# An attention block and a quantised feed-forward network on one core: the opening of the kernel in another order, and four later places

## The chip, the core and the metric

The kernel runs on one core of one Trainium2 chip. A core has five engines that run side by side: PE (TensorE, matrix products), DVE (VectorE), ACT (ScalarE), POOL (GpSimd) and SP (SyncE, which here only issues DMA transfers). They meet through semaphores. Each engine works through its own list of instructions in order, so an instruction that waits holds up all that stand behind it. The metric is the device time of one execution in microseconds (us); lower is better.

## The reference

The input `x` is 16 batches of 100 tokens of 512 numbers; `ctx` is 16 batches of 361 rows of 256. All is float32.

```
x = x + attention(layernorm(x), ctx)
        q = xn @ Wq, k = ctx @ Wk, v = ctx @ Wv      16 heads of 128
        q, k = rmsnorm(q) * gq, rmsnorm(k) * gk
        softmax(q k^T / sqrt(128)) v, then @ Wo
x = x + ffn(layernorm(x))
        gate, up (4096 x 512), down (512 x 4096) as 4-bit codes with scales
        gelu(x @ gate^T) * (x @ up^T) @ down^T
```

## The kernel before, in words

Every float32 operand of a matrix product is split into a high and a low part (`..._hi`, `..._lo`), and each product is three passes: high by high, high by low, low by high (`matmul3`, line 399). The high part is a cast, mostly on ACT (`hi`, line 791); the low part is a subtraction on DVE (`lo`, line 1158) or POOL.

The attention part runs in 64 units. A unit is one batch with one quad of four heads. Four units with the same quad and four batches (`GB`) share their queries; `quad` counts these groups of four units from 0 to 15, `i` is the unit inside its group, and `v` the unit inside the 16 that belong to the same four batches. In a unit PE does, in this order: the scores of the unit, the keys of the next unit (`keys`), the transposes of the attention weights (`transpose_attn`, line 467), two products with the context rows (`attend`, lines 482 to 488), and the transposes of the next unit's keys (`transpose_keys`, line 459). Between these stand products that belong to the group: the queries of the next quad (`query`), the values and the outputs of the quad before (`value_of`, `output`). `attend` needs the transposed weights back from ACT (high part) and DVE (low part).

Before unit 0 there is an opening: four batches of `x` are loaded, normalised (`ln1_moments`, a reciprocal root by POOL in `ln_rstd`, `ln1_normalise`), transposed by PE (`norm_transposed`, line 498) and split (`norm_hi` on ACT, `ln1_lo` on DVE, semaphore `xl`). The key weights `wk` and the head weights `head_w` are split too (`head_hi` on ACT, `head_lo` on POOL, line 1809). The first query waits until all four batches are split.

The order on every engine is written out by hand, in one function per engine. In the unit loop the POOL splits the fresh head weights (`split_head`, lines 1697 and 1699) for products that PE takes soon after. The weights of the feed-forward network are decoded in steps that are put into the last attention units (`decode` on DVE, lines 1338 to 1349). SP issues the transfers in order too, with waits in between: a head weight is loaded into one of two buffers when the one in it has been split, and each split weight is stored to memory for later quads.

## Time and profile before

| | before |
|---|---|
| median of 3 runs | 2015.75 us (2015.48 to 2016.67) |
| the profiled execution, its own time | 2015.15 us |
| span of its instructions | 2013.4 us |
| PE busy | 1968.3 us, 98% of the span |
| DVE, ACT, POOL busy | 79%, 50%, 57% |
| mean granted clock of PE | 0.993 |

The profiled execution is 1.75 us longer than its span and 0.6 us under the median. PE stood still for about 45 us of the span. The rows below are from views that list instructions in order of time for one engine, with the idle time before each and what ended it, and from views that sum up a stretch.

### The profile page before, as it was taken

How to read it: one execution, taken by the hardware profiler on the slowest of the kernel's cores; microseconds unless marked ns; L12 is line 12 of the kernel's file. 1: busy time of each engine (PE TensorE's matmuls, PEld its weight loads, DVE VectorE, ACT ScalarE, POOL GpSimd, SP SyncE). 2: the span in 40 equal slices, each digit the busy share in tenths (PEclk: the TensorE clock that was granted, in tenths of full speed). 3: DMA queues.
4: the chain of work that ended last, by engine and by line, in shares of the span. 5: the costliest groups of instructions: out<-in, count | busy, mean ns of one | idle time of the engine just before them, and what ended most of it. 6: DMA issues, size and time to landing. Idle time of an engine off the chain costs nothing.

```text
span 2013.4 us, 34243 instructions
## 1 busy us (share of the span) xinstructions
PE 1968.3 (98%) x11504; PEld 1894.8 (94%) x11504; DVE 1596.6 (79%) x3034; ACT 1000.4 (50%) x2322; POOL 1152.1 (57%) x1305
## 2 busy tenths in 40 slices
PE   6999999999999999999999999989999999999998
PEld 5899899999999999999999999979999999999998
DVE  6777787778877778877788877888888888888875
ACT  4555455555555555555555552344444444444442
POOL 6756656532444433434332335688888888887771
PEclk9999999999999999999999999989999999999999
DMA  6434434333332333332322424111111111111001
GB/s 187 135 111 153 145 120 143 111 119 95 114 118 88 125 105 92 122 113 93 118 90 85 144 78 135 47 49 32 32 32 33 41 33 33 32 32 33 32 1 66
DMA packets 93500, 174.57 MB, mean 87 GB/s; under 512 B 13249, under 2 KB 49745, under 8 KB 91281
## 3 DMA queue, kind: packets, MB, share of 16 engines
q1 hardware_dynamic: 93328, 172.39, 26.8%
q8 instruction: 95, 1.56, 0.3%
q14 instruction: 77, 0.62, 0.1%
HBM read 139.00 MB, written 33.36 MB: 86 GB/s over the span
## 4 chain that ended last, share of the span: by engine, by line
PE 89%; DVE 6%; ACT 1%; issue 1%; POOL 1%; DMA 1%; SPq 0%; DVEq 0%; POOLq 0%; ACTq 0%
PE psum L402 43%; PE psum L743 21%; PE psum L435 6%; PE psum L482 3%; PE psum L467 3%; PE psum L459 3%; PE psum L488 3%; PE psum L483 3%; PE psum L532 2%; DVE tT_lo L1158 1%; PE psum L498 1%; DVE kaT_lo L1158 0%; DVE xT_lo L1158 0%; DVE g L1366 0%; DVE work L1264 0%
## 5 line engine op out<-in xcount | busy, mean ns | idle before, releaser
L1158 DVE TENSOR_TENSOR kaT_lo<-psum,kaT_hi 128x488 fp32r<-128x488 f32 (+2 forms) x384 | 216.1, 613 | 51.9 <-ACT kaT_hi L791 51.8
L851 ACT ACTIVATE work<-psum,stats,q_rstd 100x361 f32<-100x361 f32 x256 | 163.6, 650 | 185.6 <-DVE stats L1255 185.6
L402 PE MATMUL psum<-wk,ctxT_hi 128*122 128x512 f32 x768 | 243.0, 398 | 2.4 <-DVE wk L1158 2.4
L1793 POOL TENSOR_TENSOR inter_lo<-g,inter_hi 128x400 fp32r<-128x400 f32 x128 | 142.1, 1114 | 132.5 <-ACT inter_hi L791 131.6
L791 ACT CAST kaT_hi<-psum 128x488 fp32r<-128x488 f32 (+2 forms) x384 | 178.8, 540 | 75.0 <-PE psum L467 73.4
L1653 POOL TENSOR_SCALAR k_ss<-k_ss 122x4 f32<-122x4 f32 x192 | 37.1, 193 | 298.4 <-DVE k_ss L1214 297.7
L1655 POOL TENSOR_TENSOR k_ss<-k_ss,power 122x4 f32<-122x4 f32 x192 | 193.8, 1009 | 16.0
L1245 DVE TENSOR_REDUCE stats<-psum 100x2 f32<-100x722 f32 x128 | 115.7, 904 | 106.7 <-PE psum L435 106.6
L402 PE MATMUL psum<-inter_hi,down_hi 128*128 128x400 f32 x512 | 176.5, 345 | 3.0 <-ACT inter_hi L791 3.0
L402 PE MATMUL psum<-inter_lo,down_hi 128*128 128x400 f32 x512 | 176.3, 344 | 0.0
L402 PE MATMUL psum<-inter_hi,down_lo 128*128 128x400 f32 x512 | 176.2, 344 | 0.0
L402 PEld LDWEIGHTS psum<-wk,ctxT_hi 128*122 128x122 f32 x768 | 140.3, 184 | 34.2 <-issue 2.7
L402 PE MATMUL psum<-xlnT_hi,head_w 128*128 128x400 f32 x512 | 150.1, 354 | 3.0 <-DVE xlnT_lo L1158 1.8
L1668 POOL TENSOR_TENSOR q_sqs_lo<-q_sq,q_sqs_hi 128x400 fp32r<-128x400 f32 x60 | 63.0, 1050 | 157.4 <-ACT q_sqs_hi L791 157.4
L402 PE MATMUL psum<-wk,ctxT_lo 128*122 128x512 f32 x384 | 152.2, 396 | 0.0
L402 PE MATMUL psum<-oT_hi,head_w 128*128 128x400 f32 x496 | 146.3, 356 | 2.6 <-POOL head_w L1699 2.6
L1399 DVE SCALAR_TENSOR_TENSOR ysum<-psum,ysum 128x400 f32<-128x400 f32 x192 | 107.6, 565 | 52.0 <-PE psum L402 51.8
L791 ACT CAST yT_hi<-psum 128x400 fp32r<-128x400 f32 x128 | 63.1, 493 | 158.8 <-PE psum L488 158.7
L482 PE MATMUL psum<-kaT_hi,ctxN_hi 122*128 122x400 f32 (+1 forms) x384 | 135.0, 352 | 4.5 <-DVE kaT_lo L1158 4.5
L964 ACT ACTIVATE g<-g 128x400 f32<-128x400 f32 x128 | 69.0, 539 | 133.0 <-DVE g L1361 132.4
L483 PE MATMUL psum<-kaT_hi,ctxN_lo 122*128 122x400 f32 (+1 forms) x384 | 132.2, 344 | 0.0
L1221 DVE TENSOR_TENSOR work<-psum,k_ss 122x512 f32<-122x512 f32 x192 | 125.5, 681 | 4.0 <-POOL k_ss L1655 3.9
(242 smaller groups left out, 6268.1 us busy)
## 6 DMA issues: line engine op xcount, KB each, us to landing
head_w<-spill_sq SPq DMA_DIRECT2D x48, 512.0 KB, 3.5
head_w<-spill_so SPq DMA_DIRECT2D x46, 512.0 KB, 3.9
wk<-spill_sk SPq DMA_DIRECT2D x12, 1024.0 KB, 5.7
wv<-spill_sv SPq DMA_DIRECT2D x48, 256.0 KB, 2.8
spill_sq<-head_w SPq DMA_DIRECT2D x16, 512.0 KB, 3.0
spill_so<-head_w SPq DMA_DIRECT2D x16, 512.0 KB, 3.0
wk_raw<-in_ctxT SPq DMA_DIRECT2D x12, 361.0 KB, 4.0
head_raw<-in_Wq SPq DMA_DIRECT2D x16, 256.0 KB, 3.8
```

The lines of the kernel that those rows point to most:

```text
L402: last = e.matmul(out, a_, b_, start=i == 0, stop=i == len(passes) - 1)
L435: last = e.matmul(bank[3 + h][0:SQ, 0:SCOLS], qT[quad % 2][h][q_][:, qs], kT[k_][:, h, 0:SCOLS], start=term == 0, stop=term == 2)
L482: e.matmul(out, nh[0:n, t, cs], aT[0][0:n, t, :], start=t == 0, stop=False)
L483: e.matmul(out, nl[0:n, t, cs], aT[0][0:n, t, :], start=False, stop=False)
L743: last = e.matmul(into, a_, b_, start=n == 0 and i in (0, 1, 3), stop=n == len(terms) - 1, skip_group_check=True)
L791: e.copy(dst, src).then_inc(S[sem], 1)
L851: e.activation(attn[h][:, 0:SKV], bank[3 + h][0:SQ, 0:SKV], ACT.Exp, bias=st[:, h:h + 1], scale=rq[:, i * QH + h:i * QH + h + 1], accum_ou ...
L1158: e.tensor_tensor(dst, src, high.bitcast(F32), ALU.subtract).then_inc(S[sem], 1)
L1221: e.tensor_tensor(khat[:, t, :].rearrange("p (h d) -> p h d", h=QH), bank[t][0:KP, :].rearrange("p (h d) -> p h d", h=QH), k_ss[u % 2][:, ...
L1245: e.tensor_reduce(st[:, 2 * p:2 * p + 2], scored(p), AX_X, ALU.max, negate=True).then_inc(S["mx"], 1)
L1655: e.tensor_tensor(c, c, power[0:KP, :], ALU.pow).then_inc(S["krs"], 1)
L1793: e.tensor_tensor(il[:, :], gact[n % 3][:, :], ih[:, :].bitcast(F32), ALU.subtract).then_inc(S["il"], 1)
```

## The change

In the opening:
- PE first does 28 transposes of the identity matrix into bank 7, which nothing reads.
- The first quad's key weights are loaded, cast and subtracted in two halves, with semaphores of their own for the first (`wah`, `wal`). The first key product starts on the first half.
- On PE two key tiles follow the transposes of the first batch, and the third follows those of the second.
- On ACT, DVE and POOL the steps on the four batches stand ahead of head weights and key sums.
- On SP the third head weight is loaded ahead of the store of the first, and the second context batch behind them.

In units 0 and 1 the query products of the second quad (heads 0 and 1) are cut in two: half stands before `attend`, half where the whole stood. In unit 2 the query of head 2 moves behind `transpose_attn`.

In unit 10 a reciprocal root on POOL (`ln_rstd(1, coming + 1)`) moves behind the first late split of a head weight. The same line touches units 26 and 42, which have no such split, and there the order stays.

In unit 61 `decode(0, 1)` on DVE moves from before `attended(u, 0)` to behind the last `transposed_keys`.

```diff
+WARM = 28
@@ tensor_program
-            def matmul3(out, terms):
+            def matmul3(out, terms, begins=True, ends=True):
...
-            for b in range(GB):
+            for n in range(WARM):
+                e.transpose(bank[7][:, 0:P], ident[:, :], ident[:, :])
+            for b, tiles in enumerate(((0, 1), (2,), (), ())):
                 e.wait_ge(S["xn1"], b + 1)
                 norm_transposed(b, 1, 3 + b)
-                if b < KT:
-                    keys(0, b)
+                for t in tiles:
+                    keys(0, t)
...
+                        if quad > 0:
+                            query(quad + 1, 2, 7)
                 transpose_attn(u)
+                if u == 0:
+                    e.wait_ge(S["qvs"], QH)
+                    query(1, 0, 7, (0, 1))
+                elif u == 1:
+                    query_evicted(1, 0)
+                    query(1, 1, 7, (0, 1))
+                elif u == 2:
+                    query(1, 2, 7)
...
+                if u < 2:
+                    query(1, i, 7, (2, 3))
@@ scalar_program
+            e.wait_ge(S["d_wa"], 16)
+            hi(wk[0][:, 0, :], wk_raw[:, 0, :], "wah")
             e.wait_ge(S["d_wk"], 16)
-            hi(wk[0], wk_raw[:, :, :], "wkh")
+            hi(wk[0][:, 1, :], wk_raw[:, 1, :], "wkh")
             norm_hi(0, 3)
+            square_keys(0, 0)
+            norm_hi(1, 4)
+            square_keys(0, 1)
             head_hi(0)
-            norm_hi(1, 4)
-            square_keys(0, 0)
+            norm_hi(2, 5)
+            square_keys(0, 2)
+            norm_hi(3, 6)
             head_hi(1)
...
@@ vector_program
-                if u == UNITS - 3:
-                    decode(0, 1)
                 attended(u, 0)
...
+                elif u == UNITS - 3:
+                    decode(0, 1)
@@ gpsimd_program
             ln_rstd(1, 1)
+            ln_rstd(1, 2)
             head_lo(0)
-            ln_rstd(1, 2)
+            ln_rstd(1, 3)
             head_lo(1)
-            ln_rstd(1, 3)
...
-                if g + 1 < NG and v in (10, 11):
-                    ln_rstd(1, coming + 2 * (v - 10) + 1)
+                if g + 1 < NG and v == 11:
+                    ln_rstd(1, coming + 3)
                 for n in late_splits(u):
...
                     split_head(n)
+                    if g + 1 < NG and v == 10 and n == late_splits(u)[0]:
+                        ln_rstd(1, coming + 1)
@@ sync_program
-            load_wk(0)
+            load(wk_raw[:, 0, :], d["Wk"][0:P, cols(0, QH * HD)], "d_wa")
+            load(wk_raw[:, 1, :], d["Wk"][P:2 * P, cols(0, QH * HD)], "d_wk")
...
             load_head(1)
+            load_head(2)
+            store_head(0)
             load_ctx("T", 1)
-            for n in range(2):
-                store_head(n)
-                load_head(n + 2)
+            load_head(3)
+            store_head(1)
```

Three places as the two programs order them. The first is DVE in the opening, before; `BN_STATS` begins the moments of one batch (semaphores `s_d_x1` to `s_d_x3` name it), `xlnT_lo` is a batch's low part, and the first row is the low part of the context.

```order
L1158 TENSOR_TENSOR ctxT_lo<-first_T,ctxT_hi 128x2x361 [waits s_ctxh]
L1171 TENSOR_SCALAR xb<-xb,ln_small 100x512 [waits s_rstd1]
L1162 BN_STATS ln_small<-xb 100x6 [waits s_d_x1]
L1164 BN_AGGR ln_small<-ln_small 100x2 [waits s_bn1]
L1166 TENSOR_SCALAR ln_small<-ln_small 100x1 [waits s_bn1]
L1158 TENSOR_TENSOR wk<-wk_raw,wk 128x1024 [waits s_wkh]
L1171 TENSOR_SCALAR xb<-xb,ln_small 100x512 [waits s_rstd1]
L1158 TENSOR_TENSOR xlnT_lo<-psum,xlnT_hi 128x4x100 [waits s_xh]
L1162 BN_STATS ln_small<-xb 100x6 [waits s_xn1,s_d_x2]
L1164 BN_AGGR ln_small<-ln_small 100x2 [waits s_bn1]
L1166 TENSOR_SCALAR ln_small<-ln_small 100x1 [waits s_bn1]
```

The same place after the change (line numbers are those of the changed program):

```order
L1196 TENSOR_SCALAR xb<-xb,ln_small 100x512 [waits s_rstd1]
L1183 TENSOR_TENSOR ctxT_lo<-first_T,ctxT_hi 128x2x361 [waits s_ctxh]
L1183 TENSOR_TENSOR wk<-wk_raw,wk 128x512 [waits s_wah]
L1183 TENSOR_TENSOR wk<-wk_raw,wk 128x512 [waits s_wkh]
L1187 BN_STATS ln_small<-xb 100x6 [waits s_d_x1]
L1189 BN_AGGR ln_small<-ln_small 100x2 [waits s_bn1]
L1191 TENSOR_SCALAR ln_small<-ln_small 100x1 [waits s_bn1]
L1183 TENSOR_TENSOR xlnT_lo<-psum,xlnT_hi 128x4x100 [waits s_xh]
L1196 TENSOR_SCALAR xb<-xb,ln_small 100x512 [waits s_rstd1]
```

The normalising of batch 0 now stands ahead of the context, and both halves of the key weights ahead of the moments of batch 1; the low part of each batch stands ahead of the normalising of the next.

The second is PE at the end of the attention transposes of unit 0, before, where `kaT` holds the transposed weights and `ctxN` the context rows of `attend`:

```order
L467 MATMUL psum<-ident,work 122x100 x2
L467 MATMUL psum<-ident,work 117x100
L482 MATMUL psum<-kaT_hi,ctxN_hi 128x400
L483 MATMUL psum<-kaT_hi,ctxN_lo 128x400
L482 MATMUL psum<-kaT_hi,ctxN_hi 128x400
```

And after, with six passes of the next quad's first query (`xlnT`, `head_w`) in between:

```order
L477 MATMUL psum<-ident,work 122x100 x2
L477 MATMUL psum<-ident,work 117x100
L403 MATMUL psum<-xlnT_hi,head_w 128x400
L403 MATMUL psum<-xlnT_lo,head_w 128x400
L403 MATMUL psum<-xlnT_hi,head_w 128x400 x2
L403 MATMUL psum<-xlnT_lo,head_w 128x400
L403 MATMUL psum<-xlnT_hi,head_w 128x400
L492 MATMUL psum<-kaT_hi,ctxN_hi 128x400
L493 MATMUL psum<-kaT_hi,ctxN_lo 128x400
```

The other six passes stay behind the key transposes, where all twelve were.

The third is POOL at the end of unit 10, before; `ln_small` is the root that moves, and the `head_w` rows behind it are the split of output weight 2 of quad 1:

```order
L1660 TENSOR_TENSOR q_rstd<-q_rstd,power 100x4 [waits s_qvs]
L1668 TENSOR_TENSOR q_sqs_lo<-q_sq,q_sqs_hi 128x400 [waits s_qss,s_qsh]
L1648 TENSOR_TENSOR ln_small<-ln_small,power 100x1 [waits s_bn1]
L1697 TENSOR_SCALAR head_w<-head_raw 128x512 [waits s_d_hs1,s_q,s_d_hw1]
L1699 TENSOR_TENSOR head_w<-head_raw,head_w 128x512 [waits s_hwh]
L1865 TENSOR_TENSOR wk<-wk_raw,wk 128x1024 [waits s_wkh]
L1697 TENSOR_SCALAR head_w<-head_raw 128x512 [waits s_d_hs0,s_out,s_d_hw0]
```

And after:

```order
L1687 TENSOR_TENSOR q_rstd<-q_rstd,power 100x4 [waits s_qvs]
L1695 TENSOR_TENSOR q_sqs_lo<-q_sq,q_sqs_hi 128x400 [waits s_qss,s_qsh]
L1724 TENSOR_SCALAR head_w<-head_raw 128x512 [waits s_d_hs1,s_q,s_d_hw1]
L1726 TENSOR_TENSOR head_w<-head_raw,head_w 128x512 [waits s_hwh]
L1675 TENSOR_TENSOR ln_small<-ln_small,power 100x1 [waits s_bn1]
L1892 TENSOR_TENSOR wk<-wk_raw,wk 128x1024 [waits s_wkh]
L1724 TENSOR_SCALAR head_w<-head_raw 128x512 [waits s_d_hs0,s_out,s_d_hw0]
```

The root has gone behind that one split; the subtraction of the key weights (`wk`) still follows both.

## Rows read from the trace of the kernel before

**Rows 1.** Timeline of PE, first 30 us (start, length, engine, line, operation [idle before <- releaser]).
```profile
8.66 0.90 PE L498 MATMUL psum<-ident,xb 100*128 100x100 f32 x4 [8.66 <-DVE xb L1171]
...
11.96 1.19 PE L402 MATMUL psum<-wk,ctxT_hi 128*122 128x512 f32 x2 [2.40 <-DVE wk L1158]
...
14.65 0.87 PE L498 MATMUL psum<-ident,xb 100*128 100x100 f32 x4
...
21.43 0.42 PE L402 MATMUL psum<-xlnT_hi,head_w 128*128 128x400 f32 x1 [1.28 <-DVE xlnT_lo L1158]
...
27.30 0.42 PE L402 MATMUL psum<-xlnT_hi,head_w 128*128 128x400 f32 x1 [1.26 <-POOL head_w L1809]
```

**Rows 2.** Timeline of the other engines over the same stretch, plus one ACT row.
```profile
3.55 0.31 POOL L1806 MEMSET first_N<- 122x256 f32 x1
...
8.39 1.05 ACT L791 CAST wk<-wk_raw 128x1024 fp32r<-128x1024 f32 x1 [1.27 <-DMA wk_raw<-in_Wk]
...
9.58 0.69 DVE L1162 BATCH_NORM_STATS2 ln_small<-xb 100x6 f32<-100x512 f32 x1 [1.07 <-DMA xb<-in_x]
...
10.60 1.22 DVE L1158 TENSOR_TENSOR wk<-wk_raw,wk 128x1024 fp32r<-128x1024 f32 x1
...
10.76 1.47 POOL L1648 TENSOR_TENSOR ln_small<-ln_small,power 100x1 f32<-100x1 f32 x1 [4.84 <-DVE ln_small L1166]
...
15.56 0.49 ACT L791 CAST xlnT_hi<-psum 128x400 fp32r<-128x400 f32 x1 [2.72 <-PE psum L498]
...
17.13 1.30 POOL L1809 TENSOR_TENSOR head_w<-head_raw,head_w 128x512 fp32r<-128x512 f32 x1 [2.21 <-ACT head_w L791]
...
18.98 0.55 DVE L1171 TENSOR_SCALAR xb<-xb,ln_small 100x512 f32<-100x512 f32 x1 [0.72 <-POOL ln_small L1648]
...
23.89 0.51 ACT L817 ACTIVATE first_sq<-psum 128x400 f32<-128x400 f32 x1 [2.04 <-PE psum L402]
```

**Rows 3.** Windows, 15 to 18 us: PE, PEld, DVE, ACT, POOL busy, PEclk, DMA, GB/s.
```profile
15.00:18.00 3.00, 3.00 (x12) 2.33 (x11) 2.36 (x6) 1.50 (x3) 0.87 (x1) 1.00 0.83 262
```

**Rows 4.** Timeline of PE, behind units 0 and 1, and one late row.
```profile
48.62 0.67 PE L482 MATMUL psum<-kaT_hi,ctxN_hi 122*128 122x400 f32 x1 [2.03 <-DVE kaT_lo L1158]
...
51.76 0.42 PE L482 MATMUL psum<-kaT_hi,ctxN_hi 122*128 122x400 f32 x1
...
53.48 1.42 PE L459 MATMUL psum<-ident,work 122*128 122x122 f32 x12
...
66.30 0.42 PE L482 MATMUL psum<-kaT_hi,ctxN_hi 122*128 122x400 f32 x1 [1.23 <-DVE kaT_lo L1158]
...
1351.41 0.45 PE L743 MATMUL psum<-xT_hi,gate_hi 128*128 128x400 f32 x1 [1.92 <-DVE g L1366]
```

**Rows 5.** Windows, 50 to 52 us.
```profile
50.00:52.00 2.00, 2.00 (x7) 1.98 (x7) 0.77 (x2) 0.00 (x1) 1.76 (x4) 0.52 0.14 46
```

**Rows 6.** Timeline of DVE, POOL and PE at the end of unit 10.
```profile
229.32 0.54 DVE L1171 TENSOR_SCALAR xb<-xb,ln_small 100x512 f32<-100x512 f32 x1
...
230.95 0.56 POOL L1648 TENSOR_TENSOR ln_small<-ln_small,power 100x1 f32<-100x1 f32 x1 [2.42 <-DVE ln_small L1166]
...
232.29 1.28 POOL L1699 TENSOR_TENSOR head_w<-head_raw,head_w 128x512 fp32r<-128x512 f32 x1
...
233.52 2.56 POOL L1865 TENSOR_TENSOR wk<-wk_raw,wk 128x1024 fp32r<-128x1024 f32 x1
...
233.82 0.67 PE L402 MATMUL psum<-oT_hi,head_w 128*128 128x400 f32 x1 [2.63 <-POOL head_w L1699]
...
237.95 0.51 PE L435 MATMUL psum<-kaT_hi,qT_hi 128*100 128x362 f32 x1
```

**Rows 7.** Timeline of DVE and PE in unit 61.
```profile
1167.84 0.69 DVE L1338 SCALAR_TENSOR_TENSOR up_packed<-up_packed 128x512 int32<-128x512 int32 x1
...
1170.58 0.68 DVE L1221 TENSOR_TENSOR work<-psum,k_ss 122x512 f32<-122x512 f32 x1
...
1171.32 0.64 PE L459 MATMUL psum<-ident,work 122*128 122x122 f32 x4 [1.55 <-DVE work L1221]
```

More of the change, by code:

```diff
@@ L63 @@
 x1p bn2 rstd2 xn2 nT2 x2 d_x2o x3h x3l d_f0 d_f1
-d_ctxT d_ctxN d_cT0 d_cT1 d_cT2 d_cT3 d_cN0 d_cN1 d_cN2 d_cN3 ctxh ctxl d_wk wkh wkl d_ks d_kl
+d_ctxT d_ctxN d_cT0 d_cT1 d_cT2 d_cT3 d_cN0 d_cN1 d_cN2 d_cN3 ctxh ctxl d_wa d_wk wah wal wkh wkl d_ks d_kl
 d_hw0 d_hw1 hwh hwl d_hs0 d_hs1 d_hl0 d_hl1
@@ L398, in tensor_program @@
         def tensor_program(e):
-            def matmul3(out, terms):
+            def matmul3(out, terms, begins=True, ends=True):
                 passes = [ab for lh, ll, rh, rl in terms for ab in ((lh, rh), (lh, rl), (ll, rh))]
                 for i, (a_, b_) in enumerate(passes):
-                    last = e.matmul(out, a_, b_, start=i == 0, stop=i == len(passes) - 1)
+                    last = e.matmul(out, a_, b_, start=begins and i == 0, stop=ends and i == len(passes) - 1)
                 return last
@@ L443, in keys @@
                     e.wait_ge(S["ctxl"], ctx_place("T", u // GU * GB + i) + 1)
-                    if i == 0 and u < GU:
+                    if u == 0:
+                        e.wait_ge(S["wah"], 1)
+                        e.wait_ge(S["wal"], 1)
+                    elif i == 0 and u < GU:
                         e.wait_ge(S["wkh"], u // GB + 1)
@@ L452, in keys @@
                 ks = cols(t, KP)
-                matmul3(bank[t][0:KP, :], [(th[:, c, ks], tl[:, c, ks], wk[0][:, c, :], wk[1][:, c, :])
-                                           for c in range(CC)]).then_inc(S["k"], 1)
+                terms = [(th[:, c, ks], tl[:, c, ks], wk[0][:, c, :], wk[1][:, c, :]) for c in range(CC)]
+                if u == 0 and t == 0:
+                    matmul3(bank[t][0:KP, :], terms[:1], ends=False)
+                    e.wait_ge(S["wkh"], 1)
+                    e.wait_ge(S["wkl"], 1)
+                    matmul3(bank[t][0:KP, :], terms[1:], begins=False).then_inc(S["k"], 1)
+                else:
+                    matmul3(bank[t][0:KP, :], terms).then_inc(S["k"], 1)
             def transpose_keys(u, t):
@@ L513, in weight_there, with query @@
                     e.wait_ge(S[f"d_hl{n % 2}"], 16 * reloaded_before(n))
-            def query(quad, h, into):
+            def query(quad, h, into, chunks=range(DC)):
                 n = PLACE["q", quad, h]
-                weight_there(n)
-                if quad % NQUAD == 0 and h == 0:
-                    e.wait_ge(S["xl"], GB * (quad // NQUAD + 1))
+                if 0 in chunks:
+                    weight_there(n)
+                    if quad % NQUAD == 0 and h == 0:
+                        e.wait_ge(S["xl"], GB * (quad // NQUAD + 1))
                 wh, wl = head_w[n % 2]
-                matmul3(bank[into][:, 0:GT], [(wh[:, cols(c, HD)], wl[:, cols(c, HD)], xlnT[0][:, c, :], xlnT[1][:, c, :])
-                                              for c in range(DC)]).then_inc(S["q"], 1)
+                last = matmul3(bank[into][:, 0:GT], [(wh[:, cols(c, HD)], wl[:, cols(c, HD)], xlnT[0][:, c, :], xlnT[1][:, c, :])
+                                                     for c in chunks], 0 in chunks, DC - 1 in chunks)
+                if DC - 1 in chunks:
+                    last.then_inc(S["q"], 1)
             def squares_summed(quad, h, into):
@@ L663, in tensor_program @@
                     norm_transposed(norm2_at(u - 1), 2, 6)
-                if i == 0 and more:
-                    if quad > 0:
-                        e.wait_ge(S["oTl"], 4 * (quad - 1) + 3)
-                    else:
-                        e.wait_ge(S["qvs"], QH)
+                if u < 2:
+                    query(1, i, 7, (2, 3))
+                elif i == 0 and more:
+                    e.wait_ge(S["oTl"], 4 * (quad - 1) + 3)
                     query(quad + 1, 0, 7)
@@ L1294, in vector_program @@
             ln1_moments(0)
+            ln1_normalise(0)
             ctx_lo(0)
-            ln1_normalise(0)
+            e.wait_ge(S["wah"], 1)
+            lo(wk[1][:, 0, :], wk_raw[:, 0, :], wk[0][:, 0, :], "wal")
+            e.wait_ge(S["wkh"], 1)
+            lo(wk[1][:, 1, :], wk_raw[:, 1, :], wk[0][:, 1, :], "wkl")
             ln1_moments(1)
-            e.wait_ge(S["wkh"], 1)
-            lo(wk[1], wk_raw[:, :, :], wk[0], "wkl")
+            ln1_lo(0, 3)
             ln1_normalise(1)
-            ln1_lo(0, 3)
             ln1_moments(2)
+            ln1_lo(1, 4)
+            ln1_normalise(2)
+            ln1_moments(3)
+            ln1_lo(2, 5)
+            ln1_normalise(3)
+            key_sums(0, 0)
+            ln1_lo(3, 6)
+            key_sums(0, 1)
+            key_sums(0, 2)
             e.wait_ge(S["d_gq"], 16)
@@ L1866, in gpsimd_program @@
                     split_head(n)
+                    if g + 1 < NG and v == 10 and n == late_splits(u)[0]:
+                        ln_rstd(1, coming + 1)
+                if g + 1 < NG and v == 10 and not late_splits(u):
+                    ln_rstd(1, coming + 1)
                 for n in value_splits(u):
```

15 lines of the change are left out of this document (1 added, 14 removed).

## The prediction

> **What bounds the kernel now.** I read three views. The page says that PE is busy for 98% of the span, so 45 us are all that a better order can win back, with what slow clock costs on top. Next I went down the timeline of PE and took each row with an idle time in brackets. They fall into few places: the opening up to 30 us, units 0 to 2, the end of unit 10, unit 61, and six or so in the feed-forward part, which the change does not touch. Last I asked the windows for the granted clock around those places. Behind the short idle times it is untouched, but behind those of 2.03 and 2.63 us, in unit 0 and in unit 10, PE runs at about half pace (0.52 of the full 2.4 GHz, the level of 1.2) for some microseconds [rows 4, 5, 6]. So an idle time can cost twice.
>
> **The opening.** PE gets its first transposes at 8.66, its first keys at 11.96, and starts the first query at 21.43, when the low part of the last batch of x is there [rows 1]. The chain that holds it is DVE with ACT, POOL and PE in turn: moments 1.02 us (9.58 to 10.60), root 0.56 or more, normalising 0.55, transposes, cast 0.49, low part 0.57 [rows 2, 6]. It is slow for two reasons. The cast of batch 1 waits 2.72 us for PE, which is still at the keys at slow pace (six in 2.69 us, 11.96 to 14.65), and the root of batch 3 stands behind the second head split of POOL (17.13 to 18.43), so that batch 3 is normalised at 18.98 only [rows 1, 2]. From there to the query are 2.45 us.
>
> After the change I step it so. Wk has landed by 8.39; its second half is cast by 8.9 (half of 1.05) and subtracted by 9.6 (half of 1.22). Batch 1 can't start sooner than its data, 9.58: no gain there. Moments to 10.65, low part of batch 0, root, batch 1 normalised at about 11.7. Each further batch costs low part, normalising and moments, 0.5 + 0.5 + 1.02 = 2.0, with some 0.25 of waiting for its root: batch 2 at 14.0, batch 3 at 16.2. Behind that stands a loop that was not there before: a key sum on DVE (0.65), which frees ACT's third square (0.5), then the cast (0.45) and the low part (0.55) with hand-overs, 2.6 in all. The query starts at 18.85, 2.6 earlier.
>
> This needs PE in time. The 28 transposes of the identity begin when POOL's constants are done, 3.86 [rows 2]. No row shows them; the nearest are twelve of 122 columns in 1.2 to 1.4 us at full pace [rows 4], so 3 us for 28 at full pace and 6 at half: over between 7 and 10. PE then has batch 0 and six key products, twice, before batch 1: 2.8 us if the clock has risen, 5.4 if not. With the risen clock it is just ahead of DVE; without it the low part of batch 1 comes 2.5 later and the gain is gone. So the bounds are 0 and 3.4 us.
>
> Late next is ACT. The second context batch is now loaded behind the third head weight and the first store, so behind POOL's first split at about 15.6. Those three are 1129 KB; 262 GB/s moved in the window of 15 to 18 [rows 3] make 4.3 us, with issue and landing about 20.6. ACT reaches its cast before the squares of the first query; they start 2.46 us after the query [rows 1, 2], so at 21.3, and the cast takes 0.8. That is even, and I take off 0.2. From there the second idle (1.26 at 27.30, for the split of the third head weight behind ACT and POOL) stays as it is, only earlier. **Opening: 2.4 us.**
>
> **Units 0 to 2.** After the attention transposes of unit 0 PE waits 2.03 us for `kaT_lo`, and then nine products take 3.14 us (48.62 to 51.76) where the next nine take 1.72 (to 53.48) [rows 4]. Six passes of the next query fit into the wait: six at 0.19 is 1.1 us. Their weights were split by POOL more than a microsecond before, and the second half of the query is shorter by as much. `attend` starts when it did, since DVE sets it: 1.1 us won. With PE idle for 0.9 instead of 2.0 I expect the clock to stay up, as it does after 1.23 and 1.55 [rows 4, 7], and not to fall as it does after 1.92 and 2.03 [rows 4]: another 1.4, bounds 0 and 1.6. In unit 1 the wait is 1.23 [rows 4], and the half query covers 1.1 of it. In unit 2 the wait has the same size (one more such row, 1.24), and a whole query covers all of it; the transposes then stand 2.2 us earlier against DVE, as far behind the scores as unit 1 has them without waiting. **Units: 1.1 + 1.4 + 1.1 + 1.2 = 4.8 us.**
>
> **Unit 10.** PE is free at 231.2 and waits 2.63 us for a head split. POOL had stood idle for 2.42 of them, until 230.95, for the moments of the next batch, with the split behind that root [rows 6]. Now the split goes first: from 228.5, for 2.0 us (until 233.57 from 231.6 before), ready at 230.5, 0.7 before PE comes. The wait goes. The output took 4.13 us (233.82 to 237.95) for twelve products, which at 0.19 are 2.3: 1.8 won. The first scores ran slow too (0.51 long at 237.95); by the ratio 3.14 to 1.72 I estimate 0.7 for them. Sum 5.1. What is late next: the key weights' low part, 2.56 us at POOL, now from 231.5 to 234.1, and PE wants it behind the output (2.3) and twelve scores (some 2.0 by the width of their rows), at 235.5; that holds by 1.4. And DVE: it normalises at 229.32 [rows 6], where POOL now subtracts for 1.28. If the two get in each other's way, DVE's chain up to the variance that the next scores wait for is up to 1.2 late. I take 0.3 off. **Unit 10: 4.8 us**, bounds 3.4 and 5.3.
>
> **Unit 61.** Four decode steps, 1167.84 to 1170.1, hold up the third key tile on DVE (1170.58), and PE waits 1.55 for it [rows 7]. Moved behind, the tile is ready at 1169.0, before PE begins to wait (1171.32 - 1.55 = 1169.8). The decode then ends 0.6 us after the next maxima could start; PE has the eighteen key products of the next unit there before it needs DVE again, so that should stay hidden; if it does not, the 0.6 are paid. **1.4 us**, bounds 0.8 and 1.6.
>
> The moved halves of Wk and the reordered loads add one issue of 0.4 us on SP, which waits for POOL anyway: nothing.
>
> **Two engines side by side.** The root of batch 1 takes 1.47 us where DVE subtracts Wk beside it (10.60 to 11.82), and 0.56 elsewhere [rows 2, 6]. The Trainium skill, "SBUF — State Buffer", section "SBUF: two separate sides", says that DVE and POOL share one pair of ports under an exclusive lock, which the first to start holds for its whole instruction; the trace agrees. By that rule the moves in units 10 and 61 each put a DVE step against a POOL step of 1.28, and the gains there would be 4.1 and 1.0 and the sum 12.3.
>
> **Sum.** 2.4 + 4.8 + 4.8 + 1.4 = 13.4 us. The profiled execution took 2015.15, so 2001.75. It is 0.6 under the median of the runs; from the median, 2002.35. I say 2002.3.
>
> **Rivals.**
> A: the clock. The identity transposes do not lift it before the keys, or it falls at unit 0 in spite of the six passes. For: at 1351.41 an idle of only 1.92 had half pace behind it, so the edge is near [rows 4]. Against: 0.9 is far from it. One of them costs 1.4 to 2.4: 2004.5; both, 2006.
> B: the later part. All later idle times are the same but come 13 us sooner. Where half pace begins may depend on when they come: one such stretch more or less is 1.4 to 1.7, so 2000.7 or 2004. The Trainium skill, "TensorE: Matmul & The Clock Gate", Part 1, says that the monitor of PE's activity runs free and isn't restarted with a kernel. By that rule this case is likely; no row of one execution can show it.
> C: the waits only move. Filling before `attend` in units 1 and 2 delays what follows, and in unit 10 the next wait is for Wk. For: DVE is busy 79%. Against: the slack worked out above. Half of the 8.5 us (2.3 + 4.8 + 1.4) would stay: 2006.5.
> D: slower. ACT blocks in order on the second context batch, which now stands behind a wait of SP for POOL. With it wait the first query's squares, the third head split and PE. It decides from a landing at 20.6, us for us; it would have to land beyond 34 to eat the gain, and at 40 the time is 2021. Against: 1.1 MB in some 5 us.
> E: the opening wins nothing, and units 10 and 61 only their lower ends: 2.4 + 1.4 + 0.6 less, 2006.7.
>
> **Chances.** The forecast (2000.5 to 2004) 0.52, A 0.17, B beyond that range 0.1, C 0.12, E 0.05, D 0.01, something better than all (below 2000) 0.03. Range 1999 to 2007. A change of under 0.2%, 4 us, can't be told from none: faster means under 2011.7. Faster 0.96, same 0.03, slower 0.01.
>
> **What the profile after would show.** PE's first query at 18.9 with no half pace at the keys; the wait before `attend` in unit 0 under 1 us with the clock at 1.00 behind it; no idle row at the end of unit 10 and none in unit 61; POOL's idle of unit 10 behind a split; ACT's second context cast not waiting for a DMA. Wrong would be: a query later than 20.5, an idle row in unit 11 before the keys of unit 12, a gap at 1.92 or less with half pace behind it, or a sum of gains up to unit 61 that the end does not show.

## The result, and where the time went

The changed kernel takes 2005.09 us, the median of 4 runs (2004.77 to 2008.39), against 2015.8 of the kernel before beside it: ratio 0.995, interval 0.9938 to 0.9962. In a second session, with 5 runs of the one and 9 of the other, it was 2006.76 (2005.77 to 2009.93) against 2015.33 (2014.1 to 2017.81): 0.996, interval 0.9947 to 0.9972. So 10.7 and 8.6 us are gained, where 13.4 were forecast. The time lies in the stated range of 1999 to 2007, but not in the 2000.5 to 2004 that the forecast itself was given. The page of the changed kernel:

```profile
span 2002.6 us, 34302 instructions
...
PE 1969.2 (98%) x11532; PEld 1893.2 (95%) x11532; DVE 1602.7 (80%) x3035; ACT 1000.6 (50%) x2323; POOL 1151.1 (57%) x1305
```

PE's busy time tells nothing here; the gain must be read place by place. I do that by one mark in each unit, the first row of DVE's maxima (`stats<-psum`), and by DVE's last sum. How much earlier than in the profile of the kernel before a mark comes, taken from mark to mark, is what a place gave:

| place | forecast | first profile |
|---|---|---|
| opening (mark of unit 0) | 2.4 | 0.64 |
| units 0 to 2 (mark of unit 3) | 4.8 | 4.85 |
| unit 10 (mark of unit 12) | 4.8 | 3.1 |
| unit 61 (mark of unit 63) | 1.4 | 1.0 |
| feed-forward part (last sum) | 0 | 1.15 |

**Opening.** PE's timeline of the changed kernel, in answer to [rows 1]:

```profile
3.92 4.72 PE L575 MATMUL psum<-ident 128*128 128x128 f32 x28 [3.92 <-POOL first_N L1833]
...
14.09 0.56 PE L508 MATMUL psum<-ident,xb 100*128 100x100 f32 x4 [0.24 <-DVE xb L1196]
16.47 0.56 PE L508 MATMUL psum<-ident,xb 100*128 100x100 f32 x4 [1.81 <-DVE xb L1196]
18.84 0.67 PE L403 MATMUL psum<-xlnT_hi,head_w 128*128 128x400 f32 x1 [1.80 <-DVE xlnT_lo L1183]
...
26.65 0.42 PE L403 MATMUL psum<-xlnT_hi,head_w 128*128 128x400 f32 x1 [0.87 <-POOL head_w L1836]
```

Windows of the same kernel (us, then busy time of PE, PEld, DVE, ACT, POOL, granted clock, DMA share, GB/s):

```profile
12.00:18.00 6.00, 2.97 (x19) 1.96 (x18) 4.45 (x11) 2.89 (x7) 2.32 (x3) 0.93 0.24 77
18.00:24.00 6.00, 5.17 (x16) 5.15 (x17) 3.98 (x7) 2.19 (x5) 3.68 (x5) 0.50 0.71 249
```

The first query begins at 18.84, where 18.85 was forecast. But PE has waited 1.81 and 1.80 us ahead of it, and from 18 to 24 us the granted clock is 0.50, the level of 1.2 GHz. The first query takes nearly twice its time, and the third query begins only 0.65 us earlier than before.

**Unit 0.** The wait ahead of the context products fell from 2.03 to 0.92 us, with the clock at 1.00 behind it, and no wait is left in units 1 and 2:

```profile
47.99 0.42 PE L492 MATMUL psum<-kaT_hi,ctxN_hi 122*128 122x400 f32 x1 [0.92 <-DVE kaT_lo L1183]
```

**Unit 10.** Output weight 2 is there when PE comes. Three new delays of PE stand around it: 0.27 us ahead of the scores, 0.49 inside the attention transposes (1.75 us, where they take 1.26 undisturbed), and 0.83 ahead of the context products. In answer to [rows 6], PE first, then DVE and POOL:

```profile
228.23 0.38 PE L436 MATMUL psum<-kaT_hi,qT_hi 128*100 128x362 f32 x1 [0.27 <-DVE q_rstd L1260]
...
234.71 1.75 PE L477 MATMUL psum<-ident,work 100*122 100x100 f32 x12
...
239.51 0.42 PE L492 MATMUL psum<-kaT_hi,ctxN_hi 122*128 122x400 f32 x1 [0.83 <-issue]
```

```profile
223.83 1.55 DVE L1196 TENSOR_SCALAR xb<-xb,ln_small 100x512 f32<-100x512 f32 x1
...
228.57 1.67 DVE L1196 TENSOR_SCALAR xb<-xb,ln_small 100x512 f32<-100x512 f32 x1
...
233.06 1.82 DVE L1289 TENSOR_SCALAR work<-work,stats 100x361 f32<-100x361 f32 x2
```

```profile
223.82 1.28 POOL L1726 TENSOR_TENSOR head_w<-head_raw,head_w 128x512 fp32r<-128x512 f32 x1
...
226.99 2.39 POOL L1892 TENSOR_TENSOR wk<-wk_raw,wk 128x1024 fp32r<-128x1024 f32 x1
...
233.06 1.30 POOL L1726 TENSOR_TENSOR head_w<-head_raw,head_w 128x512 fp32r<-128x512 f32 x1
```

Read the two side by side: each of the three DVE rows lies beside a POOL subtraction and ends 0.3 to 0.9 us behind that one's end (0.9 where POOL's next operation, 229.35 to 229.96, follows at once). The normalising step took 0.54 us before [rows 6], and the pair of attention normalisations 0.73.

**Unit 61.** The wait of 1.55 [rows 7] is gone. The decode, now ahead of the next maxima, runs into the same thing:

```profile
1163.14 1.61 DVE L1365 SCALAR_TENSOR_TENSOR up_packed<-up_packed 128x512 int32<-128x512 int32 x1
...
1166.32 0.90 DVE L1270 TENSOR_REDUCE stats<-psum 100x2 f32<-100x722 f32 x1
```

```profile
1162.91 1.29 POOL L1762 TENSOR_TENSOR gate_lo<-wide,gate_hi 128x512 fp32r<-128x512 f32 x1 [4.17 <-ACT gate_hi L814]
```

The step took 0.69 before [rows 7]. The maxima, whose scores end at 1164.8, start 1.5 us late.

### The profile page after: what moved, and what is told of

Its sections match the earlier page's. It is cut to its first block, busy times and chain, and to the rows that moved or that the text cites. A ratio compares the mean times of both kernels' runs of the same rounds, so it can differ in the third digit from the quotient of the medians.

```text
span 2002.6 us, 34302 instructions
## 1 busy us (share of the span) xinstructions
PE 1969.2 (98%) x11532; PEld 1893.2 (95%) x11532; DVE 1602.7 (80%) x3035; ACT 1000.6 (50%) x2323; POOL 1151.1 (57%) x1305
## 4 chain that ended last, share of the span: by engine, by line
PE 89%; DVE 7%; POOL 2%; ACT 1%; issue 1%; DMA 0%; SPq 0%; DVEq 0%; POOLq 0%; ACTq 0%
PE psum L403 43%; PE psum L766 20%; PE psum L436 6%; PE psum L469 3%; PE psum L492 3%; PE psum L477 3%; PE psum L498 3%; PE psum L493 3%; PE psum L545 2%; DVE tT_lo L1183 1%; PE psum L508 1%; DVE g L1393 1%; DVE work L1289 0%; DVE ysum L1426 0%; DVE kaT_lo L1183 0%
```

## The experiments

All are edits of the changed kernel. The table gives each one's marks, how many us later (+) or earlier (-) than in the first profile of the changed kernel, and the median of its runs. In three sessions the kernel before took 2016.5, 2015.34 and 2015.33.

| kernel | unit 0 | unit 3 | unit 12 | unit 63 | last sum | median |
|---|---|---|---|---|---|---|
| open_old | +0.6 | +0.6 | +0.6 | +0.6 | +0.7 | 2005.49 |
| no_warm | +0.9 | +1.0 | +1.0 | +1.0 | +1.3 | 2006.52 |
| fill | -1.7 | -1.7 | -1.7 | -1.7 | -0.2 | 2004.26 |
| fill_ctx | -1.3 | -1.3 | -1.3 | -1.3 | -1.1 | 2004.08 |
| queries_old | +0.1 | +4.9 | +4.9 | +4.8 | +6.3 | 2013.2 |
| root_decode_old | +0.2 | +2.9 | +4.8 | +5.8 | +6.2 | 2010.25 |
| narrow | -0.1 | +0.7 | -1.6 | -2.4 | -1.2 | 2005.08 |
| best | -1.2 | -1.2 | -2.2 | -2.9 | -3.0 | 2002.69 |
| after_again | +0.6 | +3.4 | +3.4 | +3.4 | +3.8 | 2006.76 |
| end_fill | +0.6 | +3.4 | +3.4 | +3.4 | +1.8 | 2004.69 |
| best2 | -2.5 | -2.5 | -3.5 | -4.2 | -4.3 | 2000.54 |
| before | +0.6 | +5.5 | +8.6 | +9.6 | +10.7 | 2015.3 to 2016.5 |
| before_again | +1.3 | +6.1 | +9.1 | +10.1 | +11.3 | one run, 2015.71 |

**open_old.** The opening of the kernel before, on every engine:

```
-            for n in range(WARM):
-                e.transpose(bank[7][:, 0:P], ident[:, :], ident[:, :])
-            for b, tiles in enumerate(((0, 1), (2,), (), ())):
+            for b in range(GB):
```

> The changed kernel (2005.1 us) with the opening of the kernel before on every engine: no warming transposes, key weights in one load, the old orders on ScalarE, VectorE, GpSimd and SyncE; queries, root and decode stay changed. Theory: the new opening is worth 0.6 us, as the first maxima of unit 0 say, because the clock falls in its two waits of 1.8 us; so 2005.7, with unit 1 and all later ones about 0.6 later than in the changed kernel. Rival: it is worth the 2.4 us of the forecast and 1.8 of these are lost again behind it, in units 0 to 2; then about 2007.5, with the difference showing at unit 1.

Every mark is 0.57 later, up to unit 63. The whole new opening is worth 0.6 us, and nothing was won there and lost behind. The rival is out.

**no_warm.** `WARM = 0`.

> The changed kernel without the 28 warming transposes. Theory: they buy a clock that is lost again before the first query. Without them the key products run at half pace, fill the two waits of 1.8 us, and the first query starts about 1.5 us later (20.3 us) but at full pace, 2.5 instead of 5.0 us long; the third query starts within 0.5 us of 26.65, and the time is 2005.1 with 0.6 either way. Rival: the transposes carry the new opening, as the forecast had it; without them the first query starts as late and still runs at half pace, and the time is 2006.5 to 2007.

The theory missed: the clock falls all the same. The rival's half pace came, and its time too (2006.52 in its 2006.5 to 2007). PE's rows:

```profile
17.32 0.56 PE L508 MATMUL psum<-ident,xb 100*128 100x100 f32 x4 [1.83 <-DVE xb L1196]
19.69 0.67 PE L403 MATMUL psum<-xlnT_hi,head_w 128*128 128x400 f32 x1 [1.80 <-DVE xlnT_lo L1183]
```

I had let slow key products fill the two waits. They stay at 1.8: DVE can't go on before PE has transposed, so its chain slips with PE. The query is 0.85 later and at half pace as well (0.50 from 19 to 25 us). By the marks the 28 transposes are worth 1.0 us at unit 3, by the medians, which are of two sessions, 1.4.

**fill** and **fill_ctx.** PE gets transposes of the identity to do in the two waits; fill_ctx also moves the load of the second context batch ahead of that of the third head weight.

```
                 for t in tiles:
                     keys(0, t)
+                for n in range((0, 0, 14, 14)[b]):
+                    e.transpose(bank[7][:, 0:P], ident[:, :], ident[:, :])
```

> The changed kernel with 14 more transposes of the identity (about 1.5 us at full pace) behind the transposes of the third and of the fourth batch, in the two waits of 1.8 us before the first query. Theory: the clock then stays up, the first two queries take 2.5 us each from 18.9, and the third begins 1.3 to 1.9 us earlier than 26.65, the lower end if ScalarE, which waits for the second context batch until 20.97, is late for the first query's squares; so 2003.2 to 2003.8. Rival: the clock falls whatever fills the gap, since the transposes count for little, or the gain is eaten by the third head weight; then 2005.1 as before, with the third query at 26.6.

> The kernel with the filled waits, and on SyncE the load of the second context batch ahead of the load of the third head weight, so that it is issued about 10 us earlier. Theory: ScalarE's cast of that batch is done before the first query ends, its squares start at once, and the third query gains the last 0.5 us: 0.3 to 0.6 us below the kernel with the filled waits alone, near 2003.0. Rival: the earlier load takes transfer time from the normalisation's inputs and the first two head weights, and the first query starts later than 18.9: equal to the kernel with the filled waits or above it.

PE's rows and a window of fill:

```profile
16.53 0.56 PE L508 MATMUL psum<-ident,xb 100*128 100x100 f32 x4 [0.30 <-DVE xb L1198]
...
18.89 0.42 PE L403 MATMUL psum<-xlnT_hi,head_w 128*128 128x400 f32 x1 [0.28 <-DVE xlnT_lo L1185]
...
24.98 0.42 PE L403 MATMUL psum<-xlnT_hi,head_w 128*128 128x400 f32 x1 [1.48 <-POOL head_w L1838]
```

```profile
18.00:24.00 6.00, 5.23 (x30) 4.68 (x28) 4.17 (x8) 3.73 (x9) 4.12 (x6) 1.00 0.72 253
```

The clock is 1.00 where it was 0.50, and the third query begins 1.67 us earlier, with the next wait (1.48, for its weight) already in front of it. This shows the cause of the missing 1.8 us. Yet the last sum is only 0.2 earlier: behind PE's last wait the half pace lasted 6.8 us here, and 3.4 in the changed kernel; and the median, 2004.26, stays above the theory's 2003.2 to 2003.8. The clock also falls once in unit 0 of fill, from 37.8 to 41.2 us, behind a wait of 0.49 in the middle of sixteen products of two columns:

```profile
38.00:41.00 3.00, 3.00 (x9) 2.26 (x8) 2.96 (x4) 2.25 (x6) 2.92 (x3) 0.50 0.34 87
```

no_warm has the same from 38.8 to 42.2. It costs fill nothing: the slower key products only use up the waits of 0.21 and 0.89 us that stand behind them in the changed kernel.

In fill_ctx ACT no longer waits for the context batch (2.22 us in fill), but its clock rose later, so that the 28 transposes took 5.68 us and not 4.78; the mark came 0.4 later than in fill. What the moved load gives is hidden by that: not settled.

**queries_old.** The three queries of the second quad whole, and where they were.

```
-                if u == 0:
-                    e.wait_ge(S["qvs"], QH)
-                    query(1, 0, 7, (0, 1))
...
-                if u < 2:
-                    query(1, i, 7, (2, 3))
+                if i == 0 and more:
```

> The changed kernel with the queries of the second quad where the kernel before has them (the three whole, at the ends of units 0 and 1 and before the attention transposes of unit 2); all else stays changed. Theory: the split queries cover waits and hold the clock, as the forecast had it, 4.8 us: the wait before the context products of unit 0 is 2.0 again, the clock falls behind it, the waits at units 1 and 2 (1.1 and 1.2 us) come back, and unit 3 begins 4.8 us later than in the changed kernel. Rival: the clock share (1.4) was a coincidence of the timing; the waits come back but the products behind the wait of unit 0 run at full pace, and unit 3 begins 3.4 us later.

PE's rows:

```profile
48.05 0.67 PE L492 MATMUL psum<-kaT_hi,ctxN_hi 122*128 122x400 f32 x1 [2.03 <-DVE kaT_lo L1175]
...
65.62 0.42 PE L492 MATMUL psum<-kaT_hi,ctxN_hi 122*128 122x400 f32 x1 [1.24 <-DVE kaT_lo L1175]
...
84.02 0.42 PE L492 MATMUL psum<-kaT_hi,ctxN_hi 122*128 122x400 f32 x1 [1.24 <-DVE kaT_lo L1175]
```

The waits are back at their old lengths and unit 3 is 4.8 us later, as the theory had it. Set against a profile in which the clock falls in unit 0 with the split queries too (after_again, below), the edit gives only 2.1 to unit 3: its clock share is not certain. The medians say less as well: queries_old is 2.1 us below the kernel before, where its last sum is 4.4 earlier. Its ten runs spread from 2010.53 to 2015.27, and one profile doesn't show where the slower ones lose.

**root_decode_old.** Root and decode where they were.

```
-                if g + 1 < NG and v == 11:
-                    ln_rstd(1, coming + 3)
+                if g + 1 < NG and v in (10, 11):
+                    ln_rstd(1, coming + 2 * (v - 10) + 1)
```

> The changed kernel with the root of unit 10's second normalisation and the second decode where the kernel before has them. The two places are 930 us apart, so one run serves for both. Theory: the root is worth the 3.1 us that stood at unit 12, the 5.1 us wait at its end coming back whole while 2.0 us of new waits go, and the decode 1.0, 1.55 back and 0.5 gone. Unit 12 and all later ones begin 3.1 us later than in the changed kernel, unit 63 4.1. Rival: the wait of the kernel before was made in part by its own late start, and now is shorter (3.9, the lower bound of the forecast): unit 12 only 1.9 to 2.5 later.

Read from unit 3 on, since unit 0 already differs: unit 12 is 1.9 later and unit 63 another 1.0. The wait is the old one, 2.62 us, but the half pace behind it ends sooner. Of this kernel and then of the kernel before, windows around the output:

```profile
230.00:233.00 3.00, 1.79 (x5) 1.81 (x6) 1.25 (x2) 0.00 (x0) 3.00 (x2) 0.64 0.41 146
233.00:236.00 3.00, 3.00 (x15) 2.97 (x15) 0.00 (x0) 0.00 (x0) 2.92 (x4) 0.79 0.46 122
```

```profile
233.00:236.00 3.00, 2.18 (x7) 2.21 (x8) 0.85 (x2) 0.00 (x0) 3.00 (x2) 0.50 0.53 175
236.00:239.00 3.00, 3.00 (x11) 2.91 (x10) 0.00 (x0) 0.00 (x0) 2.92 (x5) 0.50 0.33 101
```

In the profiles of the kernel before it lasts 6.8 us and in this one 3.4. So moving the root is worth 3.1 or 1.9, by how the clock falls. The 1.9 is the rival's number, but not by its reason: it expected a shorter wait, and the wait came back whole.

**narrow.** Four POOL subtractions in units 10 and 11 cut to 8 columns a row, gate_lo one unit later.

```
-                e.tensor_tensor(wl[:, :], raw[:, :], wh[:, :].bitcast(F32), ALU.subtract).then_inc(S["hwl"], 1)
+                e.tensor_tensor(wl[:, 0:w], raw[:, 0:w], wh[:, 0:w].bitcast(F32), ALU.subtract).then_inc(S["hwl"], 1)
```

> The changed kernel with the four GpSimd subtractions beside VectorE's SBUF operations cut to 8 columns of each row (two head weights and the key weights in unit 10, one head weight in unit 11; the low parts of these weights are left out), and the subtraction of gate_lo that stands beside the moved decode issued one unit later, whole. Theory: VectorE's operations were held by GpSimd on the shared SBUF access: the normalisation of 1.55 and the one of 1.67 us take 0.5 to 0.8 again, the attention normalisation x2 of 1.82 takes 0.73, the first decode operation of 1.61 takes 0.69; the waits of 0.27, 0.26 with 0.49, and 0.83 us go, so unit 12 begins 1.4 to 1.9 us earlier than in the changed kernel and unit 63 another 0.5. Rival: VectorE's own queue made the waits, since it has the moments and the normalisation before the first maxima now without a pause: its operations may shorten, but unit 12 gains less than 0.5.

DVE's rows that answer to the four slow ones, and PE's transposes:

```profile
224.52 0.54 DVE L1196 TENSOR_SCALAR xb<-xb,ln_small 100x512 f32<-100x512 f32 x1
...
228.25 0.54 DVE L1196 TENSOR_SCALAR xb<-xb,ln_small 100x512 f32<-100x512 f32 x1
...
232.43 0.72 DVE L1289 TENSOR_SCALAR work<-work,stats 100x361 f32<-100x361 f32 x2
...
1161.44 0.68 DVE L1365 SCALAR_TENSOR_TENSOR up_packed<-up_packed 128x512 int32<-128x512 int32 x1
```

```profile
234.66 1.26 PE L477 MATMUL psum<-ident,work 100*122 100x100 f32 x12
```

All four are back, no PE wait is left there, and from unit 10 to 12 it gains 2.3 us (0.69 later becomes 1.64 earlier), from 61 to 63 another 0.75. The rival is out; the theory's 1.4 to 1.9 was low. So the new waits are POOL's hold on DVE, and unit 10 would have given 5.4 us without it: the forecast's 5.1 and the 0.3 taken off for this were 5.4 and 2.3 in truth. That POOL is done sooner in narrow is not what helps: in the changed kernel no row of DVE, ACT or PE between 222 and 241 us waits for POOL. The Trainium skill, "SBUF — State Buffer", section "SBUF: two separate sides", has this as an exclusive lock, which a two-port VectorE operation or one with two SBUF inputs, and a GpSimd operation, hold for a whole instruction. The trace agrees: DVE's rows that read PSUM beside the subtraction of 2.39 us (`kaT_lo`, 1.23 us for two and 0.66 for one) take as long as in narrow, where it is cut; the SBUF rows don't.

**after_again** and **before_again.** The two kernels unaltered, profiled once more.

> The changed kernel itself, nothing altered, profiled once more. Theory: part of what stands between two profiles is the execution's and not the kernel's: the stretches at half pace (behind the wait of 0.9 us in unit 0, behind the last wait of 2.96 us, near 1335 to 1345 us) fall otherwise with the same instructions, as the narrow-subtraction run and the run with root and decode undone showed a half pace in unit 0 that the first profile of the changed kernel did not have. So this profile's milestones differ from the first one's by 0.5 us or more at one of these places and by nothing elsewhere, and its times spread over 2 to 4 us. Rival: each kernel has its own fixed pattern, given by when its waits fall; then this profile repeats the first within 0.1 us at every unit, and the 1.15 us of the later part is the change's.

> The kernel before, profiled once more. Theory as for the repeat of the changed kernel: milestones differ from the first profile only where a stretch at half pace falls otherwise (units 0 to 2 by up to 0.8 us, unit 10 to 12 by up to 1.2, the end by up to 1.7). Rival: it repeats the first profile within 0.1 us everywhere.

The changed kernel's second profile is 5.2 us longer than its first (span 2007.8). Its rows:

```profile
3.92 6.02 PE L575 MATMUL psum<-ident 128*128 128x128 f32 x28 [3.92 <-POOL first_N L1833]
...
46.08 0.49 PE L477 MATMUL psum<-ident,work 100*122 100x100 f32 x3 [0.36 <-DVE work L1289]
...
46.61 0.34 PE L403 MATMUL psum<-xlnT_lo,head_w 128*128 128x400 f32 x1
...
47.17 0.54 PE L403 MATMUL psum<-xlnT_lo,head_w 128*128 128x400 f32 x1
...
48.61 0.67 PE L492 MATMUL psum<-kaT_hi,ctxN_hi 122*128 122x400 f32 x1 [0.57 <-DVE kaT_lo L1183]
```

```profile
48.00:52.00 4.00, 3.43 (x11) 3.39 (x11) 2.76 (x6) 0.49 (x3) 3.67 (x7) 0.50 0.24 76
```

And the same window in the first profile:

```profile
48.00:52.00 4.00, 4.00 (x25) 3.96 (x26) 3.32 (x6) 0.93 (x3) 3.67 (x7) 1.00 0.23 76
```

The same 28 transposes take 6.02 and not 4.72 us, since the clock rises later (+0.6 at unit 0). Then it falls in unit 0: from 0.34 to 0.54 a product, in the middle of the half query (another +2.8 by unit 3). The wait behind is shorter for it, 0.57. Ahead of the fall both profiles have the same waits, 0.21 to 0.23, 0.89 and 0.36, and in the first no fall comes, nor behind the 0.92. From there to unit 63 the two run alike, +3.4; the feed-forward part adds 0.4 and the landing of the last store 1.3. So the theory held in the main: the difference is the execution's. But the later rise at the start and the later landing of the last store were not among its places. The Trainium skill, "TensorE: Matmul & The Clock Gate", Part 1, says that the activity monitor runs free and that one kernel is therefore measured with different numbers of slow products; this pair of profiles agrees. The kernel before, profiled again, repeats its first profile but for 0.6 in the opening, where Wk was there later (a wait of 3.31 and not 2.40 for it). For that pair my theory found nothing; its timed runs still spread from 2013.23 to 2017.81.

**end_fill.** Transposes of the identity in PE's last wait.

```
+            e.wait_ge(S["uadd"], 3 * PAIRS)
+            for n in range(24):
+                e.transpose(role_bank(1, PAIRS - 1, "c")[:, 0:P], ident[:, :], ident[:, :])
             for d in range(8):
```

> The changed kernel with 24 more transposes of the identity (about 2.6 us at full pace) in the last wait of 2.96 us, ahead of the last eight down products, into a product bank whose sum has been taken. Theory: the last products run at half pace for 3.4 us (once 6.8) because of that wait; filled, the clock stays up, and the time is 1.6 us below the changed kernel's, 2003.4. Rival: the clock falls all the same, or the transposes delay the first of the eight: 2005.0 to 2005.5.

PE in the changed kernel, first profile, and in end_fill:

```profile
1988.96 0.42 PE L403 MATMUL psum<-inter_hi,down_hi 128*128 128x400 f32 x1 [2.96 <-ACT inter_hi L814]
...
1990.51 0.54 PE L403 MATMUL psum<-inter_lo,down_hi 128*128 128x400 f32 x1
```

```profile
1989.21 2.78 PE L811 MATMUL psum<-ident 128*128 128x128 f32 x24
1992.35 0.42 PE L403 MATMUL psum<-inter_hi,down_hi 128*128 128x400 f32 x1 [0.36 <-ACT inter_hi L817]
```

Up to the last wait this profile is that of after_again (+3.4); its last sum is at +1.8. The products there run at 0.34 throughout, and 1.6 us are gained, as expected. In runs it is 2004.69 against 2006.76 beside it.

**best** and **best2.** What the runs pointed to, put together. Of best2:

```
-WARM = 28
+WARM = 12
...
+                for n in range((6, 0, 14, 14)[b]):
+                    e.transpose(bank[7][:, 0:P], ident[:, :], ident[:, :])
...
-            query(0, 0, 7)
             head_hi(2)
+            query(0, 0, 7)
...
+                if u == 10:
+                    split_head(late_splits(u)[0])
                 if i >= 2 and more:
                     query_squares_lo(quad + 1, i)
...
-                    decode_lo(1)
                     decode_scaled(2)
                 elif u == UNITS - 2:
+                    decode_lo(1)
```

> The changed kernel with the two waits before the first query filled (14 transposes each), the second context batch loaded ahead of the third head weight, ScalarE's split of the third head weight ahead of the first query's squares, GpSimd's first late weight split of unit 10 ahead of its query squares (GpSimd waits 2.1 us there), and the gate_lo subtraction one unit later. Theory: opening 1.7, 0.2 and 1.2 more, as the third query's wait of 1.3 to 1.5 for its weight goes; unit 10 another 1.0 or more, since the first normalisation is no longer beside a GpSimd subtraction; 0.5 at unit 62: about 4.5 us by unit 63, and 2000.6, give or take the 1.5 by which the feed-forward part moves. Rival: the clock takes its share back, the later part giving up to 1.5 more or less, and unit 10's waits stay since the key-weight subtraction then lies beside the second normalisation: 2.9 us by unit 63, 2002.

> The best version so far (both opening waits filled, second context batch and third head weight's split earlier, unit 10's first late split ahead of the query squares, gate_lo later) with 12 warming transposes ahead of the first batch's transposes and 6 behind them instead of 28 ahead, GpSimd's split of unit 11's early weight ahead of the root of the third query, and the last wait filled. Theory: the first batch's transposes start at 6.4 instead of 8.5 to 9.7 us, so the opening gains up to 1.0 and no longer hangs on when the clock rises; unit 11's attention normalisation takes 0.9 instead of 1.8 us and the wait of 0.83 goes, 0.8 to 1.2 more at unit 12; the end 1.6: 2000 us, 2.7 below the version before it. Rival: the clock then rises later, the key products run in part at half pace and eat the start's gain; and the end takes as long as before: 2002.

best gains 2.9 by unit 63 and 3.0 at the end: 1.2 in the opening, 1.0 in unit 10, 0.7 at gate_lo. That is the rival's number, and part of its reason holds: the second normalisation, still beside the subtraction of the key weights, takes 1.69 us. The third query still waits 1.17 us; POOL has the root of the second key tile to do first. best2 takes 2000.54 us (1999.68 to 2003.2), ratio 0.9927 to the kernel before, interval 0.9915 to 0.994; that is below the changed kernel's every run. Its opening gains 2.5, as the first batch's transposes start at 6.53. From unit 63 to the last sum it gains nothing against the first profile, in spite of the filled last wait, for the reason given below under the later part. In unit 11 the wait of 0.83 did not go:

```profile
228.96 1.12 DVE L1285 TENSOR_TENSOR stats<-stats,q_rstd 100x2 f32<-100x2 f32 x1
...
230.68 0.72 DVE L1294 TENSOR_SCALAR work<-work,stats 100x361 f32<-100x361 f32 x2
```

```profile
228.76 1.31 POOL L1731 TENSOR_TENSOR head_w<-head_raw,head_w 128x512 fp32r<-128x512 f32 x1
```

```profile
236.03 0.42 PE L492 MATMUL psum<-kaT_hi,ctxN_hi 122*128 122x400 f32 x1 [0.84 <-issue]
```

The moved subtraction left the attention normalisation alone (0.72 for the pair) and held a multiplication of two numbers a row instead (1.12, where 0.16 is its usual time), on which the exponentials wait. There the theory failed: up to unit 12 best2 gains 1.0 behind its opening, as best does.

## Why the prediction was right, and where it was not

Three terms were too high, by 1.8, 1.7 and 0.4 us, and 1.15 us came in a part for which nothing was forecast. That the time lies in the range is in part luck: the errors partly cancel, and 2005.09 is nearest to rival A's 2004.5. Two of the forecast's own signs went against it: a gap of under 1.92 us with half pace behind it, and a wait of ACT's second context cast for a DMA.

- **Opening, 2.4 forecast, 0.6 measured: the term that failed.** The chain of DVE, ACT and POOL was stepped rightly, the query began at 18.84. The step that failed is "this needs PE in time": it asked for the clock at the keys only. Batches 2 and 3 come 2.4 us apart and PE has 0.6 us to do for each, so it waits 1.8 twice, and the query meets half pace. The forecast named idle times of 1.92 and 2.03 as ones behind which the clock falls, and did not look for them in the order that it had just worked out. fill shows it: 1.7 us come with the waits filled.
- **Units 0 to 2, 4.8 forecast, 4.85 in the pair of first profiles and against queries_old.** The three fills, 3.4 in sum, are in every profile of the changed kernel's order. The clock share of 1.4 is not, so that the term was met in the first pair is luck: in after_again, end_fill, root_decode_old and narrow the clock fell in the half query, behind the three short waits that the kernel before has too (0.36 the last). Rival A had this with "it falls at unit 0 in spite of the six passes"; where the half pace lasts 6.8 us the edit gives 2.1 (4.9 less 2.8), and 4.1 in narrow, where it lasts 3.4.
- **Unit 10, 4.8 forecast, 3.1 measured.** The moved root does take the wait away. The 0.3 for "if the two get in each other's way" was the mis-sized term: the lock was named, weighed at 0.7 and 1.2, and cost 2.3. It struck three times and not once. The longest row, the attention normalisation, was not looked at: before, POOL's subtraction of unit 11 (239.69, 1.30 us long) had ended 1.7 us ahead of it (242.67); now DVE is 9.6 us earlier and POOL 6.6, and both start at 233.06. One reading was wrong but did no harm: POOL's idle time of 2.42 us ends at 230.95, so it lies ahead of PE's wait, which begins at 231.19, and not inside it.
- **Unit 61, 1.4 forecast, 1.0 measured** (1.0 again with the decode undone). The lock at the first decode step makes the maxima 1.5 late and the transposes of unit 62 take 1.74 and not 1.26 us. The sum by the page's rule, 1.0, was right here.
- **Later part, 0 forecast, 1.15 in one pair.** This was rival B. Nearly all of it is one stretch at half pace. It follows the wait of 1.92 us that ends at 1351.41 [rows 4] and not the same one (1.09 us, at 1341.80) of the changed kernel; before, then after:

```profile
1352.00:1356.00 4.00, 4.00 (x16) 3.95 (x15) 3.41 (x6) 2.70 (x6) 2.55 (x3) 0.57 0.01 3
```

```profile
1342.00:1346.00 4.00, 4.00 (x23) 4.00 (x23) 3.87 (x7) 2.83 (x6) 2.90 (x3) 1.00 0.01 3
```

From there to the end of PE's last wait pass 648.3 us in both profiles of the kernel before, but also in narrow and best2, and 647.1 or 647.2 in the ten others. So it is not the change's alone; with two profiles of the kernel before, more can't be said.
- **D**, the block on ACT, did not decide: ACT waits 2.37 us for the context batch, until 20.97 where 20.6 was worked out, which hides behind the slow query.

What stays open: what makes the clock fall in unit 0 in one execution of the same instructions and not in another. In all four profiles with the fall it comes 37.55 us behind the first rise, to the hundredth. In best the clock rose as late as in after_again (9.36 and 9.59), but its unit 0 comes 1.8 us sooner, and nothing fell; in the first profile of the changed kernel it rose 2.7 us sooner and nothing fell. In fill and no_warm the fall in unit 0 came 30.7 and 27.3 us behind the first rise, and behind other waits. So it seems to hang on when the short waits come, counted from the rise. That is read from the profiles at hand and was not tried by moving the waits alone.

## What to carry to other kernels

When a reordering makes an engine earlier, write down the waits that the new order leaves, and price each of them twice: as time, and as a fall of PE's clock behind it. Fill such waits with work that nobody needs, if there is no other (1.7 us for the two in the opening, 1.6 for the last). Before a POOL operation on SBUF is moved, look which DVE operations on SBUF will stand beside it; the short ones in a chain cost as much as the long ones. And profile the same kernel twice before giving a difference of 1 to 3 us to an edit.

## What was not expected of the hardware

- Two profiles of the same instructions differ by 5.2 us of 2005: 0.6 by the rise of the clock at the start, 2.8 by its fall in unit 0, 0.4 later, and 1.3 by the landing of the last store (4.4 against 3.0 us behind the start of the last sum).
- Waits of 0.21, 0.89 and 0.36 us within 3 us are followed by a clock of 0.50 in four profiles; in the first profile of the changed kernel, in open_old, fill_ctx, best and best2 by 1.00, though 0.92 follow on them. In fill and no_warm the clock fell behind a single wait of 0.49 and 0.48 us.
- DVE's multiplication of 100x2 numbers took 1.12 us beside a POOL subtraction, and 0.16 alone: the wait is for the end of POOL's instruction, whatever the size of DVE's.
- Half pace between 1295 and 1335 us costs nothing: the products at 1297.39, 1312.33 and 1334.51 follow each other at 14.94 and 22.18 us in the changed kernel and at 14.95 and 22.19 in fill, with other stretches at half pace between them. The waits ahead of these products are ended by DVE and POOL rows (3.03, 4.51 and 1.82 us in the changed kernel), and slower products only shorten such waits.
